# Windowed attention on one core: a third query buffer, and another order of the transfers on SP's queue

## What is computed

```
x = x + conv_layer(layer_norm(x))        # this layer
t = x + ffn_layer(layer_norm(x))         # spectral mixer, after it

conv_layer: 49 windows of 8 x 8 pixels in an image
  q, k, v   = window pixels @ qkv_w + qkv_b
  lepe      = 3 x 3 depthwise convolution of v
  r_idx     = the 4 windows whose mean key fits the mean query of this window best
  k_sel, v_sel = keys and values of those 4 windows (256 pixels)
  attn      = softmax(q @ k_sel^T / 8) for each of 8 heads of 8 channels
  out       = (attn @ v_sel + lepe) @ wo_w + wo_b
```

## Time and profile before

| | us |
|---|---|
| three timed runs: median (lowest, highest) | 5104.29 (5091.42, 5108.30) |
| the profiled execution | 5097.64 |
| its span | 5095.8 |
| PE busy in the span | 3893.3 (76%) |
| DVE busy | 2444.2 (48%) |
| ACT busy | 2311.8 (45%) |
| POOL busy | 1200.6 (24%) |
| mean granted TensorE clock, full speed being 1 | 0.851 |

### The profile page before, as it was taken

How to read it: one execution, slowest core, us unless ns; L and a number is a source line. 1 busy time by engine, 2 the same in 40 slices (tenths; PEclk the granted TensorE clock), 3 DMA queues, 4 the chain that set the end, 5 groups by cost and what they waited for, 6 DMA issues and landing times. The chain is left out here.

```text
span 5095.8 us, 164212 instructions
## 1 busy us (share of the span) xinstructions
PE 3893.3 (76%) x52926; PEld 2762.2 (54%) x52926; DVE 2444.2 (48%) x4011; ACT 2311.8 (45%) x5133; POOL 1200.6 (24%) x4157
## 2 busy tenths in 40 slices
PE   4257777777777877777777777778849899999889
PEld 1135555454554545555554554556622288888779
DVE  2255565565456556555655654565525233333311
ACT  1125555555555655555565555556723233333300
POOL 0023343233233323333332332234410000000000
PEclk9998788889878988887898888789965599999955
DMA  2323333333333333333333333333258634434486
GB/s 78 106 59 105 93 88 95 103 81 87 104 93 84 99 103 82 90 104 90 85 99 103 83 84 105 93 87 63 41 72 128 111 79 100 106 88 105 95 182 166
DMA packets 824005, 486.39 MB, mean 95 GB/s; under 512 B 535753, under 2 KB 797258, under 8 KB 818794
## 3 DMA queue, kind: packets, MB, share of 16 engines
q1 hardware_dynamic: 763874, 409.35, 36.0%
q10 hardware_dynamic: 59360, 67.44, 4.5%
HBM read 265.86 MB, written 210.80 MB: 94 GB/s over the span
## 5 line engine op out<-in xcount | busy, mean ns | idle before, releaser
L902 DVE TENSOR_REDUCE Mx<-ps 128x2 f32<-128x512 f32 x1568 | 1061.4, 688 | 640.5 <-PE ps L1144 633.1
L547 POOL COPY Ksel<-Kexp 96x128 int32 x3136 | 879.6, 322 | 2043.1 <-PE ps L1166 1206.7
L746 ACT ACTIVATE Pr<-ps 128x1024 f32<-128x1024 f32 x784 | 800.6, 1021 | 923.0 <-PE ps L1166 907.6
L1144 PE MATMUL ps<-Ksel,Qbd 96*128 96x256 bf16 x3136 | 668.9, 299 | 518.8 <-DMA Qbd<-q_dram 388.4
L676 ACT ACTIVATE Vsel<-Vpx 64x72 f32 x3136 | 816.9, 260 | 307.8 <-issue 158.9
L1164 PE MATMUL ps<-Qbd,Ksel 96*128 96x128 bf16 x6272 | 903.4, 233 | 27.5 <-issue 27.0
L1166 PE MATMUL ps<-MT,each 84*128 84x128 bf16 x6272 | 902.3, 233 | 0.0
L1164 PEld LDWEIGHTS ps<-Qbd,Ksel 96*128 96x128 bf16 x6272 | 663.8, 106 | 115.1 <-issue 104.9
L1166 PEld LDWEIGHTS ps<-MT,each 84*128 84x128 bf16 x6272 | 663.9, 106 | 103.3 <-issue 94.5
L1144 PEld LDWEIGHTS ps<-Ksel,Qbd 96*128 96x128 bf16 x3136 | 214.0, 100 | 801.2 <-issue 728.8
L1183 PE MATMUL ps<-Pr,Vsel 128*9 128x64 f32 x25088 | 553.1, 234 | 78.5 <-ACT O L684 61.5
(11 more groups left out here) (165 smaller groups left out, 3630.9 us busy)
## 6 DMA issues: line engine op xcount, KB each, us to landing
q_dram<-Pq SPq DMA_DIRECT2D x336, 112.0 KB
k_dram<-Pk SPq DMA_DIRECT2D x336, 112.0 KB
Kexp<-k_dram ACTq DMA_DIRECT2D x112, 336.0 KB, 4.3
Qbd<-q_dram SPq DMA_DIRECT2D x224, 168.0 KB, 6.5
Vpx<-v_dram ACTq DMA_DIRECT2D x112, 252.0 KB
s_dram<-S SPq DMA_DIRECT2D x8, 2048.0 KB, 12.4
Sin<-s_dram SPq DMA_DIRECT2D x32, 512.0 KB, 5.7
z_dram<-Zs SPq DMA_DIRECT2D x128, 128.0 KB, 4.1
```

The costliest lines, as they stand in the source:

```text
L547: nc.gpsimd.tensor_copy(dst[:, w, :, k, :], src[:, :, bass.ds(win[k] * (PX // 2), PX // 2)])\
L746: nc.scalar.activation(Pr[k][:].rearrange("q c p h x -> q (c p h x)"), ps[:, ST0 + 2 * k:ST0 + 2 * k + 2, :].rearrange("q a b -> q (a b)") ...
L902: nc.vector.tensor_reduce(Mx[u % 2][:, 2 * half:2 * half + 2, w], ps[:, half, :].rearrange("q (p k) -> q p k", p=2), AX.X, ALU.max).then_i ...
L1144: last = mm(ps[:, half, (p % 2) * KEYS:(p % 2) * KEYS + KEYS], query(u, w, p), Ksel[u % 2][0:QROWS, w, p, :, :].rearrange("r k x -> r (k x ...
```

## The change

1. There are three `Qbd` tiles; `Q_BUF` says which one a unit uses. `load_q` for unit u+2 is issued at the end of slot u. Unit 0 of the next duo is asked for at the start of slot 13 and unit 1 at the start of slot 0.
2. The sums go from `O` straight to `sums`, with one transfer from SBUF to SBUF, and `sums_dram` is gone.
3. On SP's queue `store_k` moves ahead of `rsums_spread`, and `load_q` stands right behind the latter.
4. The input row (`load_x`) and the row with halo (`load_vh`) are asked for at the end of the slot ahead of the one that uses them.
5. To make room for the third tile, `Lp` (sum of the taps) lies on `XT` (input row), and `Sq2` on `Sq`; for that, `square`, `square2`, `tap` and `load_x` wait for each other's readers.
6. `Vt` is laid out by image first, so that one transfer with rows of 504 elements stores it where there were two with rows of 72.

```diff
+Q_BUF = [0, 1, 2, 0, 1, 2, 0, 1, 2, 0, 1, 2, 0, 1]
+Q_USES = [5, 5, 4]
+        Lp = XT
-        Lp = sb("Lp", [128, ROW])
-        Sq2 = sb("Sq2", [128, ROW])
+        Sq2 = Sq
-        Vt = sb("Vt", [PX, NWIN, 2 * HEADS, HD + 1])
+        Vt = sb("Vt", [PX, 2, NWIN * HEADS, HD + 1])
-        Qbd = [sb(f"Qbd{m}", [QROWS, HP, NWIN, 2, PX], BF16) for m in range(2)]
+        Qbd = [sb(f"Qbd{b}", [QROWS, HP, NWIN, 2, PX], BF16) for b in range(3)]
...
             def load_x(e, i):
                 hold(sp, "sp", cen_ready, e * NWIN + i)
+                if i == 0:
+                    hold(sp, "sp", conv_ready, e * NWIN)
...
             def load_q(d, u):
-                par, m = u % 2, u // NWIN
+                b, m = Q_BUF[u], u // NWIN
...
-            def sums_to_dram(g, m):
+            def sums_spread(g, m):
                 hold(sp, "sp", o_copied, g * 2 + 2)
-                sp.dma_start(sums_dram[m], O[m][HD:128:32].rearrange("j w a q -> j (w a q)")).then_inc(sums_out, 16)
-
-            def sums_spread(g, m):
-                hold(sp, "sp", sums_out, g * 16 + 16)
-                sp.dma_start(sums[:, :], sums_dram[m].rearrange("j (p x) -> (j p) x", p=32)).then_inc(sums_in, 16)
+                hold(sp, "sp", rsums_ready, g)
+                sp.dma_start(sums[:, :], O[m][HD:128:32].rearrange("j w a q -> j (w a q)")).then_inc(sums_in, 16)
...
             def slot(d, u, first, last):       # SP
-                if prev and not (last and u == UNITS - 1):
-                    if u == UNITS - 1:
-                        hold(sp, "sp", q_stored, (e + 1) * (6 * 16 * NWIN))
+                if u == 0:
+                    if prev:
+                        hold(sp, "sp", st_ready, g * NWIN)
+                        load_q(d, 1)
+                    if not last:
+                        load_x(e, 0)
+                if u == UNITS - 1 and not last:
+                    hold(sp, "sp", q_stored, (e + 1) * (6 * 16 * NWIN))
                     hold(sp, "sp", st_ready, g * NWIN)
-                    load_q(d if u < UNITS - 1 else e, (u + 1) % UNITS)
-                if not last and u <= LAST:
-                    load_x(e, u)
+                    load_q(e, 0)
...
-                if conv:
-                    load_vh(e, u - NWIN)
-                    if u > NWIN:
-                        store_conv(e, u - NWIN - 1)
+                if conv and u > NWIN:
+                    store_conv(e, u - NWIN - 1)
...
                 if prev:
-                    sums_to_dram(g - 1, (u - 1) % 2)
+                    sums_spread(g - 1, (u - 1) % 2)
...
-                if prev:
-                    sums_spread(g - 1, (u - 1) % 2)
...
+                if behind:
+                    store_k(e, u - 1)
                 if prev:
                     rsums_spread(g - 1, (u - 1) % 2)
-                if behind:
-                    store_k(e, u - 1)
+                if u < UNITS - 2:
+                    hold(sp, "sp", st_ready, g * NWIN)
+                    load_q(d, u + 2)
+                if not last and u < LAST:
+                    load_x(e, u + 1)
+                if not last and LAST <= u < UNITS - 1:
+                    load_vh(e, u - LAST)
...
-            def square2(t):
+            def square2(t, after):             # POOL
                 hold(pool, "pool", cen2_ready, t + 1)
+                hold(pool, "pool", var_ready, after)
```

More of the change, by code:

```diff
@@ L239, in attention @@
         xp_loaded = sem("xp_loaded")
-        q_loaded = [sem(f"q_loaded{m}") for m in range(2)]
+        q_loaded = [sem(f"q_loaded{b}") for b in range(3)]
         k_gathered = sem("k_gathered")
@@ L508, in _ @@
             store_x2(d, NWIN - 2)
-            sums_to_dram(duos * UNITS - 1, 1)
             sums_spread(duos * UNITS - 1, 1)
@@ L593, in slot @@
                     if w == 3 and u <= LAST and not last:
-                        square(e * NWIN + u)
+                        square(e * NWIN + u, e * NWIN - 9 + min(u, 2))
                     if w == 4 and load is not None:
-                        square2(load[0] * NWIN + load[1])
+                        square2(load[0] * NWIN + load[1], e * NWIN + (0 if last else min(u, LAST) + 1))
             def body(d, first, last):
@@ L602, in _ @@
             bodies(pool, body)
-            square2(tiles - 2)
-            square2(tiles - 1)
+            square2(tiles - 2, tiles)
+            square2(tiles - 1, tiles)
         @block.scalar
@@ L887, in tap @@
                     hold(dve, "dve", conv_ready, t)
+                    if i == 0:
+                        hold(dve, "dve", cen_ready, t + NWIN)
                     nc.vector.tensor_scalar(out, src, taps[:, 0:1], None, ALU.mult).then_inc(tap_done, 1)
@@ L962, in _ @@
                 for k in range(9):
-                    tap(i, k)
+                    tap(i, i, k)
                 add_conv(i)
@@ L1025, in slot @@
                         for _ in range(TAPS_AT[w]):
-                            tap(ct, count)
+                            tap(ct, u - NWIN, count)
                             count += 1
@@ L1088, in values_t @@
                 hold(pe, "pe", s, value)
+                nw = 4 - sub
+                out = ps[0:PX, MISC, 0:nw * 128].rearrange("q (m w c) -> q m w c", m=2, w=nw)
                 for w in range(4 * sub, 4 + 3 * sub):
-                    last = mm(ps[0:PX, MISC, w % 4 * 128:w % 4 * 128 + 128], Xn[:, w * PX:w * PX + PX], wv[:, :],
-                              start=True, stop=True)
+                    last = mm(out[:, :, w % 4, :], Xn[:, w * PX:w * PX + PX], wv[:, :], start=True, stop=True)
                 last.then_inc(vt_ready, 1)
@@ L1133, in query @@
             def query(u, w, p):
[L1134 removed]
+                return Qbd[Q_BUF[u]][0:QROWS, p, w, :, :].rearrange("r h x -> r (h x)")
             def scores(d, n, u, w, half):
```

48 lines of the change are left out of this document (22 added, 26 removed).

## The result

The changed kernel takes 4992.8 us (median of four runs, 4985.77 to 4994.8) against 5106.3 (four runs, 5091.42 to 5134.0): a ratio of 0.9774, 95% interval 0.975 to 0.9798. It is faster by 2.3%. The forecast was 4900, in a range of 4690 to 5085. The profiled execution took 4994.8 us.

A forecast was written before the change was run, and what follows sets the result against it. PE was taken as busiest, held by late `Qbd` loads, with DVE waiting for `VH`. Seven duos at -25.1 us (-176) and the last duo (-19), from 5097.6, gave 4903, stated as 4900; range 4690 to 5085.

The forecast's parts named there:

- rival A: Slots 1 to 7: `Rb` waits for the key stores, at 84 GB/s; 4790 to 5020 us, chance 0.55.
- The other step: Third query buffer: the load gets about 25 us of room, so its wait costs 0 in slots 2 to 12.
- B: Keys don't hold `Rb`: slots 2 to 7 fall to 25.3 us, total 4507; chance 0.13.
- D: Slower than before: bursts drain slowly and SP's queue never empties; 5160 us with `normalise` at 26 us; chance 0.12.
- C: Bursts drain slower than in the preparation, ACT's loads sharing engines: `normalise` after 24.3 us, total 5079; chance 0.20.
- First query store to `normalise`: Slots 1 to 7: twelve stores ahead of `Rb` make this 20.7 us, where it was 14.5.
- The 84 GB/s: DMA rate read from the preparation's twelve stores, taken for both bursts ahead of `Rb`: 1.376 MB in 16.4 us.
- Slots 9 to 12: Convolution slots with `VH` in time take 24.5 us; slot 9 saves 1.8, slots 10 to 12 save 4.6 each.
- Slot 8: No key or query stores, but starts after a gap: 28.0 us, saving 6.4.
- Slot 13: Query load of unit 0 still goes out at its start; with `VH` a slot ahead it saves 2.1 us.
- The load for u+2 goes out a whole slot ahead of need: Third query buffer: a transfer 7.4 us late then has about 25 us of room.
- The last duo: Three slots with a gap for `Qbd` save 6.4 us each, 19 us, against 20.3 us for a slot without.

The follow-up runs named there:

- e1: Changed kernel with the six key stores put back behind the spread into `Rb` on SP's queue: 4898.0 us, ratio 0.9593.
- e5: Kernel before with only the key stores moved ahead of the spread into `Rb`, still two query buffers: 5177.1 us, ratio 1.0130.
- e7: Changed kernel with each key store issued a second time, to a tensor that nothing reads: 5590.5 us, ratio 1.0942.
- e9: Changed kernel with the halo row load back at the start of its own slot, three query buffers kept: 5088.3 us, ratio 0.9959.
- e4: Kernel before with only the halo row load moved to the end of the slot ahead: 5142.3 us, ratio 1.0075.
- e8: Changed kernel with the key stores last in the slot, behind query load, input row and halo row: 4913.9 us, ratio 0.9624.
- e10: As e1, but the query load for unit u+2 is issued at the start of slot u: 4838.0 us, ratio 0.9459.
- e12: As e10, with two buffers for the first key part and the key stores last in the slot: 4810.2 us, ratio 0.9434.

## Why the prediction was right, and where it was off

**The mechanism** was rival A, the forecast, in its main step: `Rb` waits behind twelve stores, and that wait takes the place of the one for `Qbd`. e1, e5 and e7 show it from three sides: keys away, keys alone, keys doubled. The other step, that the third buffer ends the wait for `Qbd`, was not borne out: with two buffers and the keys first 68.1 us of it are left (e5), with three buffers and the keys behind the spread 326.6 (e1). It is mainly the keys' new place that ended it. B (the keys don't hold `Rb`, 4507) and D (5160) are out. The measured time lies between A and C: A put `normalise` 20.7 us after the first query store, C 24.3, and it is 22.1 in the mean of 49 slots.

**The size** was off by 93 us. The sum by slots in duo 2, forecast and measured:

| | before | forecast | measured |
|---|---|---|---|
| slots 1 to 7 | 239.0 | 238.0 | 250.3 |
| slot 8 | 34.4 | 28.0 | 25.1 |
| slots 9 to 12 | 114.1 | 98.0 | 97.5 |
| slot 13 | 28.7 | 27.0 | 30.7 |
| together | 416.2 | 391.0 | 403.6 |

In the kernel before, slot 13 runs from 1617.68 to 1646.38; the forecast took the mean of slots 10 to 13, 29.1, for it. The forecast's 25.1 us a duo were 12.6 in this duo. The missing 12.5 us over seven duos are 88, which is nearly all of the 93. That is not quite the account of the whole program: in the mean of duos 1 to 6 only 10.1 us were saved in these slots, and the 2.4 us of slot 0, which the forecast had at nothing, make up for it.

*First query store to `normalise`: 20.7, measured 22.4 in slot 2 and 22.1 in the mean of 49 slots.* This is the term that carries the miss; with 12.2 us from `project` to the first query store (1246.19 to 1258.41, forecast 12.1) and 1.24 from `normalise` to `project` it makes a period of 35.9 in slot 2 and not 34.0. The times of the DMA packets in the trace divide it. The first packet of the stores moves 1.3 us after the first query store, both bursts take 18.8 us from their first packet to their last, and `normalise` follows 2.0 us later (means of 49 slots). The forecast had 0.9, then 17.4 (16.4 for the stores and 1 for `Vs`), then 2.4. So what I mis-sized is the drain of the two bursts, the time until their last packet has moved.

*The 84 GB/s* of the earlier trace rows come from the preparation, where the same twelve stores took 16.1 us from first packet to last. In slot 2 of the change the queries kept that pace (1259.68 to 1268.20, 8.5 us for 0.688 MB) and the keys did not (1268.68 to 1278.94, 10.3 us, so 67 GB/s). Over the first half of the keys, ACT's load of `Kexp`, 0.344 MB, was moving as well (1268.66 to 1273.73). That is rival C's reason, at part of its size; no run took that load away, so it is argued and not shown. It also means that the end of an issue is not the end of a burst: SP had issued `Rb` 17.1 us after the first query store (1275.54 less 1258.41), and the key packets ended at 20.5.

*Slot 1* was the one place where a loss was forecast (4.4 us), and it came: 29.60 to 34.33, 4.7.

*Slots 9 to 12* at 24.4 us each were forecast at 24.5. *Slot 8* came out 2.9 us better: its clock is 0.88, and I had taken slot 9's of before, 0.85, and added 1.7 for work and clock that weren't lost.

*Slot 13: 27.0, measured 30.7.* Here a step failed. "Slots 13 and 0 keep what they have", I wrote, and still took 2.1 us off slot 13. But `load_vh` of slot 13 now stands at the end of slot 12, where it holds for that slot's last tap, and the query load of unit 0 stands behind it:

```profile
1586.11 0.37 SPq L389 DMA_DIRECT2D VH<-vimg_dram  x1
1586.90 4.12 SPq L364 DMA_DIRECT2D Qbd<-q_dram  x2
```

```profile
1596.39 0.59 PE L1151 MATMUL ps<-Ksel,Qbd 96*128 96x256 bf16 x2 [4.73 <-DMA Qbd<-q_dram]
```

I named what is queued behind `Rb`, and not what is queued behind `VH`. e9 confirms it: with `load_vh` back at the start of its slot, PE's waits for `Qbd` fall from 38.2 us in 8 places to 4.8 in 2. e4 is the same fault in every convolution slot.

**"The load for u+2 goes out a whole slot ahead of need": wrong, with little effect on the time.** The scores run six windows ahead, so those of window 0 of unit u+2 stand in slot u+1 at w = 1. A load at the end of slot u has a window or two, not 25 us. It was in time because no burst stood between the spread and it: slots 9 to 12 of duo 2, in which DVE never waits for `Rb`, have no wait for `Qbd` either, and in e8, with `Rb` in time and the keys behind the query load, that wait stays at 40.0 us. In e1 the keys stand between the two, and 326.6 us of waits are back. In slots 1 to 7 of the change PE's stand-still for `Rb` gave the load more room besides (in e8 that for L1091 may do the same); whether it was needed there was not tried. A real slot of lead (e10) is worth 60 us there.

**The last duo.** It had three long slots, 25.9 to 26.8 us, in the kernel before and has one (23.6 us) now; twelve of its slots take 234.17 us, 19.5 each, at a clock of 0.99. The forecast had 20.3.

```profile
3392.30:3626.47 234.17, 207.03 (x4439) 154.15 (x4439) 140.11 (x229) 182.76 (x431) 100.97 (x383) 0.99 0.25 50
```

**Still open.** How far the waits could be brought down at best: the fastest version still has 201.8 us of waits for `Rb`. The first `project` of the program is 9.8 us later, where the forecast had 4.4 for the first slot 1; e1, with the keys behind the spread, has it at 376.9 and not 384.7, so most of it is the keys again. A split of the bursts between two queues was not tried. Nor was a free tile for unit 0 of the next duo, which might take the 4.7 us out of slot 13.

## What to carry to other kernels

A burst of stores that fills a queue makes late whatever stands behind it; moving it changes the victim. Here it was the query load (388.4 us of waits), then the reciprocals (447.6), then the buffer that the stores read (246.4, e8), then the value store (133.7, e12). So before moving a burst, list for each transfer behind it when its data, or its buffer, is needed next, and put the burst ahead of the one with the most room. A further buffer gives a load more room only if the load is also issued earlier: with three buffers and the load at the slot's end 326.6 us of waits were left (e1), with the load at its start 39.9 (e10).

A transfer that must wait for a semaphore is a wait for everything behind it. The same edit (the halo row one slot ahead) cost 0.75% with the query load behind it and gave 1.9 points with the query load ahead of it. Judge such edits together, not one by one.

## What the runs showed that I had not expected

The wait of a small transfer behind a burst has two parts, and only one is the queue. Moved to the other engine's queue, the spread overtook the keys, but it still took 5.35 us from issue to use while they were moving, against 2.4 us without them.

A burst's rate was not the same everywhere in the kernel. Six stores of 0.688 MB moved at some 84 GB/s in the preparation and at 81 as queries in slot 2, at 67 as keys in the same slot, and at 54 as the second keys of e7.

The longer slots came with a lower clock. In duo 2 the changed kernel's slots 2 to 7 spend fewer us busy on PE than before (151.37 against 152.93) and take 6.5 us more, and their mean clock is 0.82 where it was 0.86.
